# A four-layer graph network on 16 pairs: separate logit products, one bank for a pair's projections, pair-wide transfers and 14 steps given to VectorE

## The chip, the cores and the metric

One Trainium2 chip, one of its NeuronCores. The metric is the time of one execution on the device in microseconds, the median of three runs: 269.04 us (268.43 to 270.58).

## What is computed

The input is x, 32 graphs of 256 nodes with 128 features each, and adj, 32 integer matrices of 256 x 256 with entries 0 and 1. Four layers follow one another, each added to its input and normalized over the features:

```python
def _L0_gnn_ref(x, adj, W, a_src, a_dst):
    h = jnp.einsum('bnf,of->bno', x, W)
    e = (h @ a_src)[:, :, None] + (h @ a_dst)[:, None, :]
    e = jnp.where(adj == 0, NEG_INF, jax.nn.leaky_relu(e, negative_slope=0.2))
    return jnp.einsum('bij,bjo->bio', jax.nn.softmax(e, axis=-1), h)
...
x = _layernorm(x + _L0_gnn_ref(x, adj, L0_gnn_W, L0_gnn_a_src, L0_gnn_a_dst), axis=-1)
x = _layernorm(x + _L1_gnn_ref(x, adj, L1_gnn_W, L1_gnn_a), axis=-1)
x = _layernorm(x + _L2_gnn_ref(x, adj, L2_gnn_a0, L2_gnn_a1, L2_gnn_a2, L2_gnn_a3, L2_gnn_bias), axis=-1)
x = _layernorm(x + _L3_gnn_ref(x, L3_gnn_adj, adj, L3_gnn_weight, L3_gnn_bias), axis=-1)
```

Layer 1 is like layer 0 with other weights. Layer 2 takes sigmoid(leaky(x a x')) as its matrix wherever adj has the value of the relation, layer 3 multiplies the adjacency of each relation with x and that with the relation's weights. Since adj holds only 0 and 1, the kernel computes one relation in layers 2 and 3, keeps note of any other entry (`seen`), and has a general path behind a branch that these inputs don't take.

## The kernel before

The 32 graphs are worked in 16 pairs ("teams", `H = 2`). For each pair a chain of some thirty steps runs over four layers; each step is a small function of one engine, and all steps are written out by hand in `ORDER`, one string per engine: `h0:5` is the step `h` of layer 0 for pair 5. An engine takes its string from left to right and never overtakes. Before each step it waits on semaphores for the steps of other engines whose result it needs, eight semaphores per engine (`K = 8`), so pairs n and n+8 share one. `BANKS` says which of the 8 PSUM banks each product uses, and `bank_free` (L979) makes PE wait for the step that last read the bank (`freed_by`, L972). Rings of buffers (`X_IN`, `XT_IN`, `ADJ`, ...) limit how far a pair may run ahead.

The steps around the change, in the order of one pair:
- SyncE (`load_xT`, `load_x`, `load_adj`, L454 to L471): three loads for each of the two graphs, x laid out by nodes, x turned, the adjacency turned; behind the ninth entry of its string three loads of later weights (L482), all four relations' weights and two biases broadcast to 128 partitions. ScalarE's queue loads W0, the eight attention columns, the turned W0, and W1 (L545 to L548).
- PE `h` (`projections`, L1000): for each graph and each half of 128 nodes one f32 product with the 128x128 block of turned x as stationary and `w_fast` of 130 columns as moving operand, 128 of features and 2 of logits. Each graph has a bank of its own, so a pair holds two. `w_fast` of layer 0 is made from W0 by a product with two columns (L966), that of layer 1 from W1 less its mean (`projection_centre`, L685, and L969, L970).
- VectorE `logits` (L721): takes the two logit columns out of the bank, an instruction for each graph. PE `dT` (L1016) turns them, VectorE `peak` takes the largest, PE `top` (L1020) spreads it, VectorE `dmax`, `shift` subtract it, ScalarE `gains` take two exponentials. `dT` and `top` write into the free columns of the bank of the pair's first projection. ScalarE `vals` (L572) copies the features out of the bank, which is then free.
- PE `rows` (L1029), VectorE `weight` (L760), PE `out` (L1070), VectorE `rsum`, `rinv`, `res` (L799), `stats` (L806), `var`; GpSimd `pow` (L525) for the reciprocal root; ScalarE `norm` (L610; L620 in layer 1, L623 in layers 2 and 3).
- Layer 2: PE `xT`, ScalarE `xTa`, PE `score` (L1037, L1038), ScalarE `sigmoid` (L597, L598), VectorE `alpha` (L767), PE `out`. VectorE adds (L791) what GpSimd `bias` (L521) made of x and the bias. Layer 3: ScalarE `high` (L603) and GpSimd `low` (L530) split x into two f16 parts, PE `agg` (L1047) gathers them, ScalarE copies (L608), PE `out` (L1067).
- VectorE `raw` (L712), `seen` (L719) and ScalarE `mask` (L555) turn the loaded adjacency into what the layers use. SyncE `store` (L473) writes each graph when its `norm3` is done.

The lines that set the cost of a projection are

```python
last = nc.tensor.matmul(place(f"h{l}", u)[:, b * HC:(b + 1) * HC], (xT_in if l == "0" else fxT)(u)[:, b * P:(b + 1) * P], w_fast[:, int(l), :],
                        start=True, stop=True)
```

## Time and profile before

| | us |
|---|---|
| runs, median (lowest, highest) | 269.04 (268.43, 270.58) |
| profiled execution | 270.16 |
| its span, first to last instruction | 268.3 |
| busy in it: VectorE / TensorE / ScalarE / GpSimd | 240.3 / 234.8 / 224.7 / 147.5 |

All times below are microseconds from the start of the profiled span unless marked ns. Engines: PE is TensorE, PEld its weight loads, which overlap it, DVE VectorE, ACT ScalarE, POOL GpSimd, SPq the queue on which SyncE issues DMAs. L1012 is line 1012 of the kernel. `x8` counts instructions of one form that follow each other; the time beside them runs from the first start to the last end. In square brackets stands how long the engine was idle before, and for whom it waited. PEclk is the share of TensorE's clock that was granted.

### The profile page before, as it was taken

The numbers are of one execution on the slowest core, as the hardware profiler recorded it, in microseconds if no ns is written. First come the engines' busy times: TensorE is split into PE (matmuls) and PEld (weight loads), VectorE is DVE, ScalarE is ACT, GpSimd is POOL, SyncE is SP. The second block draws the span as 40 slices with busy tenths as digits, with TensorE's granted clock in tenths as the row PEclk, the third lists the DMA queues.
The fourth block names the chain that finished last, engine by engine and source line by source line (L and its number), as shares of the span: only waits on it lengthen the run. The fifth ranks groups of instructions, "written<-read, shape, count | busy, mean of one in ns | idle before, by whom it ended". The sixth has DMA issues, their size and how long they took to land.

```text
span 268.3 us, 6075 instructions
## 1 busy us (share of the span) xinstructions
PE 234.8 (88%) x1799; PEld 206.9 (77%) x1799; DVE 240.3 (90%) x917; ACT 224.7 (84%) x656; POOL 147.5 (55%) x167
## 2 busy tenths in 40 slices
PE   1796789999999999898899999999999989988960
PEld 1685578798878988788887888988989878877740
DVE  1886999999999899999999999999899998996481
ACT  2431855898989899889997999899899979999984
POOL 1002111605946456866196344798632697899992
PEclk9979999999999999999999999999999999999995
DMA  6979190021280402831106101500020100010114
GB/s 183 366 64 279 42 300 16 19 99 42 78 277 3 120 0 53 247 133 43 42 2 195 39 2 40 156 4 0 23 98 2 40 4 0 0 42 1 39 50 154
DMA packets 20115, 22.12 MB, mean 82 GB/s; under 512 B 2288, under 2 KB 15984, under 8 KB 20080
## 3 DMA queue, kind: packets, MB, share of 16 engines
q1 hardware_dynamic: 19504, 21.50, 27.0%
q8 instruction: 16, 0.26, 0.4%
q10 hardware_dynamic: 576, 0.20, 0.3%
q14 instruction: 19, 0.16, 0.2%
HBM read 17.50 MB, written 4.19 MB: 81 GB/s over the span
## 4 chain that ended last, share of the span: by engine, by line
DVE 54%; POOL 12%; PE 9%; ACT 8%; issue 8%; DMA 6%; SPq 1%; ACTq 1%; DVEq 0%; POOLq 0%
DVE wgt_all L760 12%; DVE fstats L806 9%; DVE fres L799 8%; POOL frstd L525 5%; POOL xb L521 4%; DMA x_in<-x_laid 4%; DVE wgt_all L767 4%; DVE fres L791 4%; DVE raw_all L712 3%; POOL fxTa L530 2%; DVE seen L719 2%; PE banks L1012 2%; ACT xs L623 2%; ACT vals_all L579 2%; DMA w_nat<-in_L_gnn_W 2%
## 5 line engine op out<-in xcount | busy, mean ns | idle before, releaser
L525 POOL TENSOR_TENSOR frstd<-fvar,minus_half 128x4 f32<-128x4 f32 x64 | 75.2, 1179 | 103.1 <-DVE fvar L812 46.6
L1070 PE MATMUL banks<-vals_all,wgt_all 128*128 128x129 f32 x512 | 63.1, 279 | 2.9 <-DVE wgt_all L760 2.9
L1070 PEld LDWEIGHTS banks<-vals_all,wgt_all 128*128 128x128 f32 x512 | 60.2, 194 | 3.8 <-issue 3.0
L760 DVE SCALAR_TENSOR_TENSOR wgt_all<-banks,gain,maskT 128x256 f32<-128x256 f32 x128 | 52.4, 474 | 0.5 <-PE banks L1029 0.3
L806 DVE BATCH_NORM_STATS2 fstats<-fres 128x6 f32<-128x256 f32 x128 | 47.7, 415 | 0.0
L623 ACT ACTIVATE xs<-fres,frstd 128x128 f32<-128x128 f32 x128 | 41.0, 413 | 1.2 <-POOL frstd L525 1.1
L1037 PE MATMUL banks<-fxT,fxTa 128*128 128x256 f32 x128 | 36.1, 384 | 0.1
L1070 PE MATMUL banks<-xs,wgt_all 128*128 128x128 f32 x256 | 32.0, 278 | 0.3
L1070 PEld LDWEIGHTS banks<-xs,wgt_all 128*128 128x128 f32 x256 | 29.9, 192 | 1.5 <-issue 1.2
L562 ACT COPY fxT<-banks 128x256 f32<-128x256 f32 x64 | 20.6, 392 | 10.9 <-PE banks L997 10.9
L791 DVE TENSOR_TENSOR fres<-banks,xb 128x256 f32<-128x256 f32 x64 | 23.7, 412 | 6.6 <-PE banks L1070 3.4
L620 ACT ACTIVATE xs<-fres,fcenter,frstd 128x128 f32<-128x128 f32 x64 | 26.5, 494 | 3.6 <-DVE fcenter L823 3.1
L530 POOL TENSOR_TENSOR fxTa<-xs,fxTa 128x256 f16<-128x256 f32 x32 | 23.0, 739 | 9.5 <-ACT fxTa L603 9.5
L521 POOL TENSOR_TENSOR xb<-xs,bias 128x256 f32<-128x256 f32 x32 | 26.2, 837 | 3.0 <-ACT xs L620 2.9
L521 POOL TENSOR_TENSOR xb<-xs,bias_up 128x256 f32<-128x256 f32 x32 | 24.1, 776 | 0.0
L1037 PEld LDWEIGHTS banks<-fxT,fxTa 128*128 128x128 f32 x128 | 19.3, 191 | 6.0 <-issue 0.3
L767 DVE TENSOR_TENSOR wgt_all<-sg_all,wgt_all 128x512 f32<-128x512 f32 x32 | 22.9, 749 | 1.2 <-ACT wgt_all L598 1.2
L579 ACT ACTIVATE vals_all<-banks,fscale 128x128 f32<-128x128 f32 x64 | 18.4, 383 | 4.8 <-DVE fscale L750 4.6
L1029 PE MATMUL banks<-ident,gain 128*128 128x128 f32 x128 | 19.5, 281 | 2.5 <-ACT vals_all L570 1.6
L1012 PE MATMUL banks<-w_fast,xT_in 128*128 128x130 f32 x128 | 19.1, 295 | 2.1 <-issue 1.6
L555 ACT CAST maskT<-adj_in 128x512 bf16<-128x512 int32 x32 | 18.4, 650 | 2.5 <-DMA adj_in<-adj_turned 2.4
L799 DVE SCALAR_TENSOR_TENSOR fres<-banks,finv,x_in 128x128 f32<-128x128 f32 x64 | 18.0, 341 | 2.4 <-DMA x_in<-x_laid 2.2
(92 smaller groups left out, 448.6 us busy)
## 6 DMA issues: line engine op xcount, KB each, us to landing
adj_in<-adj_turned SPq DMA_DIRECT2D x32, 256.0 KB, 3.8
xT_in<-x_turned SPq DMA_DIRECT2D x32, 128.0 KB, 3.3
x_in<-x_laid SPq DMA_DIRECT2D x32, 128.0 KB, 3.4
out<-xs SPq DMA_DIRECT2D x32, 128.0 KB, 1.7
w<-in_L_gnn_weight SPq DMA_DIRECT2D x1, 256.0 KB, 3.9
bias<-in_L_gnn_bias SPq DMA_DIRECT2D x2, 128.0 KB, 9.4
w_nat<-in_L_gnn_W ACTq DMA_DIRECT2D x2, 64.0 KB, 3.8
w_fast<-W_turned ACTq DMA_DIRECT2D x1, 64.0 KB, 4.4
```

The source lines that it names most:

```text
L521: nc.gpsimd.tensor_tensor(xb(u)[:, :, :], xs(u)[:, :, :], bias_up[:, :, :] if l == "3" else bias[:, 0, :, :], ALU.add).then_inc(fast_pool[ ...
L525: nc.gpsimd.tensor_tensor(frstd[:, int(l), slot(n), :], fvar[:, int(l), slot(n), :], minus_half[:, :, :], ALU.pow).then_inc(fast_pool[k], 1)
L530: nc.gpsimd.tensor_tensor(lo(u)[:, :, :], xs(u)[:, :, :], hi(u)[:, :, :], ALU.subtract).then_inc(fast_pool[k], 1)
L620: last = nc.scalar.activation(xs(u)[:, b, :], fres(u)[:, b, :], ACT.Identity, bias=fcenter[:, u, b:b + 1], scale=frstd[:, 1, u, b:b + 1])
L623: last = nc.scalar.activation(xs(u)[:, b, :], fres(u)[:, b, :], ACT.Copy, scale=frstd[:, int(l), u, b:b + 1])
L760: last = nc.vector.scalar_tensor_tensor(out=wgt(u)[:, c, :], in0=place(f"rows{l}", u), scalar=gain[:, u, c, 1:2], in1=maskT(u)[:, c, :], o ...
L767: nc.vector.tensor_tensor(wgt(u), sg(u), wgt(u), ALU.max).then_inc(fast_dve[k], 1)
L791: nc.vector.tensor_tensor(fres(u)[:, :, :], place(f"out{l}", u).rearrange("p (b c) -> p b c", b=NB), xb(u)[:, :, :], ALU.add).then_inc(fas ...
L799: last = nc.vector.scalar_tensor_tensor(out=fres(u)[:, b, :], in0=sums[:, b, 0:D], scalar=finv[:, u, b:b + 1], in1=(x_in if l == "0" else ...
L806: nc.vector.bn_stats(fstats[:, u, :, :].rearrange("p b k -> p (b k)"), fres(u)[:, :, :].rearrange("p b d -> p d b")).then_inc(fast_dve[k], 1)
L1037: nc.tensor.matmul(place("score", u)[:, c * N:(c + 1) * N], fxTa(u)[:, c * P:(c + 1) * P], fxT(u)[:, :], start=True, stop=False)
L1070: last = nc.tensor.matmul(place(f"out{l}", u)[:, b * width:(b + 1) * width], wgt(u)[:, c, b * P:(b + 1) * P], (vals if l in "01" else xs)( ...
```

## The change

The logits get products of their own: a step `lg` multiplies the same stationary blocks of turned x with the last two columns of `w_fast`, all four products of a pair into one bank, in which `dT` and `top` also work. The projection `h` moves 128 columns only, both graphs of a pair into one bank; it no longer stands between x and the logits, and its result is needed by `vals` alone. `logits` takes the four columns pairs with one instruction.

Loads and stores move a pair at a time, from inputs laid out for it. W0 and the eight columns come as one load. The biases are laid out for 128 partitions beforehand and come as one load, and of layer 3's weights only the used relation; both stand behind the twelfth entry of SyncE's string. The mean of W1 is taken after the first `shift` and the weights of layer 1 are made before the first `weight` (PE: before the first `rows`).

VectorE gets versions of `mask`, `bias`, `low` and `norm`, and 14 steps of other engines now stand in its string: `mask:10`, `norm2` of 5, 8, 11, 12, 14, `norm3` of 10, 14 (from ScalarE), `low` of 9, 13, 14, 15, `bias2:15`, `bias3:12` (from GpSimd). Waits for such a step ask `doer` which engine has it. All five strings and `BANKS` are written anew. In ScalarE's string the runs of `gains` and of `sigmoid` alternate 18 times, before 16 times.

```diff
 ORDER = {
     "sp": (
-        "xT:0 adj:0 adj:1 xT:1 adj:2 xT:2 adj:3 x:0 xT:3 x:1 adj:4 x:2 xT:5 adj:5 x:4 adj:6 adj:7 x:3 xT:4 x:6 x:5 "
-        "adj:8 xT:6 xT:9 x:9 adj:11 xT:7 adj:9 xT:8 adj:10 adj:12 x:7 xT:12 xT:11 x:10 xT:10 x:8 adj:14 adj:13 x:11 "
...
+        "xT:0 xT:2 xT:1 adj:0 adj:1 xT:3 x:0 adj:2 xT:4 xT:5 adj:4 x:2 adj:5 adj:3 x:1 xT:6 x:4 adj:6 xT:7 adj:7 "
+        "adj:8 x:5 x:6 x:3 adj:9 xT:10 adj:12 x:9 adj:11 xT:9 xT:8 x:7 adj:10 adj:13 x:8 xT:11 store:1 store:0 "
...
     "pe": (
-        "h0:0 dT0:0 h0:1 top0:0 dT0:1 top0:1 rows0:0 rows0:1 out0:0 out0:1 xT1:0 h0:2 h1:0 dT0:2 xT1:1 h0:3 dT1:0 "
...
+        "lg0:0 h0:0 dT0:0 lg0:2 lg0:1 top0:0 dT0:1 top0:1 dT0:2 rows0:0 h0:1 h0:2 rows0:1 out0:0 lg0:3 lg0:4 h0:4 "
+        "dT0:3 dT0:4 top0:2 xT1:0 h0:3 top0:3 top0:4 lg1:0 h1:0 dT1:0 out0:1 top1:0 lg0:5 rows0:2 rows1:0 out0:2 "
...
     "dve": (
-        "raw:0 logits0:0 peak0:0 raw:1 seen:0 seen:1 logits0:1 dmax0:0 shift0:0 peak0:1 dmax0:1 raw:2 shift0:1 "
...
+        "logits0:0 peak0:0 logits0:1 dmax0:0 shift0:0 logits0:2 peak0:1 raw:0 dmax0:1 seen:0 shift0:1 raw:1 weight0:0 "
+        "weight0:1 rsum0:0 raw:2 logits0:3 logits0:4 rinv0:0 peak0:2 res0:0 peak0:3 stats0:0 peak0:4 var0:0 dmax0:2 "
...
+        "res2:15 stats2:15 low:13 var2:15 res3:11 alpha:14 stats3:11 var3:11 res2:14 stats2:14 var2:14 low:15 res3:12 "
+        "norm2:14 stats3:12 low:14 res3:13 var3:12 stats3:13 res3:15 var3:13 stats3:15 var3:15 res3:14 stats3:14 "
+        "var3:14 norm3:14"
...
-    "h0": "01 23 23 40 16 23 71 75 40 32 67 67 32 73 46 67",
...
+    "h0": "1 5 6 3 7 3 4 6 6 2 4 0 1 2 1 0",
+    "lg0": "0 3 2 4 5 5 7 6 4 2 5 0 3 7 0 6",
...
-PHASES = {"h0": H, "rows0": 1, "out0": H, "xT1": 1, "h1": H, "rows1": 1, "out1": H,
+PHASES = {"lg0": 1, "h0": 1, "rows0": 1, "out0": H, "xT1": 1, "lg1": 1, "h1": 1, "rows1": 1, "out1": H,
...
-        loads = [
-            (w3[:, :, :], W3.rearrange("r d o -> d r o")),
-        ]
-        for k, bb in ((0, bias2), (1, bias3)):
-            loads.append((bias[:, k, :, :], bb.rearrange("(a c d) -> a c d", a=1, c=1).to_broadcast([P, NB, D])))
+        loads = [(bias[:, :, 0, :], biases_laid), (w3[:, 0, :], W3[0])]
         WEIGHTS = 16 * len(loads)
+        LOADS_AFTER = FIRST_LOADS
...
             def load_xT(l, n, k):
-                for u in graphs(n):
-                    if n >= XT_IN:
-                        sp.wait_ge(fast_pe[(n - XT_IN) % K], at("pe", "h0", u - XT_IN * H))
-                    sp.dma_start(xT_in(u)[:, :], x_turned[u]).then_inc(fast_xT_in[u % (XT_IN * H)], 16)
+                if n >= XT_IN:
+                    sp.wait_ge(fast_pe[(n - XT_IN) % K], max(at("pe", "h0", final(n - XT_IN)), at("pe", "lg0", final(n - XT_IN))))
+                sp.dma_start(xT_all[:, pair(n, XT_IN), :], x_turned[n]).then_inc(fast_xT_in[n % XT_IN], 16)
...
             def store(l, n, k):
-                for u in graphs(n):
-                    sp.wait_ge(fast_act[k], at("act", "norm3", u))
-                    sp.dma_start(out[u], xs(u)[:, :, :]).then_inc(fast_stored[n % XS], 16)
+                normer = doer("norm3", n)
+                sp.wait_ge(signals[normer][k], at(normer, "norm3", final(n)))
+                sp.dma_start(out[n * H:(n + 1) * H].rearrange("h p b d -> p h b d"), xs_all[:, pair(n, XS), :, :]).then_inc(fast_stored[n % XS], 16)
...
-            act.dma_start(w_nat[:, 0, :], W0).then_inc(w0_in, 16)
-            act.dma_start(columns[:, :], vector_columns).then_inc(columns_in, 16)
+            act.dma_start(w0_pack[:, :], W0_and_columns).then_inc(w0_in, 16)
             act.dma_start(w_fast[:, 0, 0:D], W0_turned).then_inc(w0_turned_in, 16)
-            act.dma_start(w_nat[:, 1, :], W1).then_inc(w1_in, 16)
+            act.dma_start(w1_nat[:, :], W1).then_inc(w1_in, 16)
...
+            def normalize(l, n, k):
+                dve.wait_ge(fast_pool[k], at("pool", f"pow{l}", n * H))
+                for u in graphs(n):
+                    for b in range(NB):
+                        last = nc.vector.tensor_scalar(xs(u)[:, b, :], fres(u)[:, b, :], frstd[:, int(l), u, b:b + 1], None, ALU.mult)
+                    last.then_inc(fast_dve[k], 1)
...
+                if f"lg{l}" in PHASES:
+                    parts = chain_place(l, n)[:, 0:H * NB * 2]
+                    if l == "0":
+                        nc.vector.tensor_copy(logit[:, 0, slot(n), :, :].rearrange("p u b k -> p (u b k)"), parts).then_inc(fast_dve[k], 1)
+                    else:
+                        nc.vector.tensor_tensor(logit[:, 1, slot(n), :, :].rearrange("p u b k -> p (u b) k"), parts.rearrange("p (c k) -> p c k", k=2),
+                                                frstd[:, 0, slot(n), :].rearrange("p u (b a) -> p (u b) a", a=1).to_broadcast([P, H * NB, 2]), ALU.mult).then_inc(fast_dve[k], 1)
+                    return
...
                 if q == 0:
                     projection_weights(0)
-                    projection_centre()
+                if q == first_weight:
+                    projection_weights(1)
                 if q == finished:
                     output_weights()
                 steps[step](l, n, n % K)
-                if q == first_logits:
-                    projection_weights(1)
+                if q == first_shift:
+                    projection_centre()
...
+                    width = HC if PHASES[f"h{l}"] == H else D
                     for b in range(NB):
-                        last = nc.tensor.matmul(place(f"h{l}", u)[:, b * HC:(b + 1) * HC], (xT_in if l == "0" else fxT)(u)[:, b * P:(b + 1) * P], w_fast[:, int(l), :],
+                        last = nc.tensor.matmul(place(f"h{l}", u)[:, b * width:(b + 1) * width], (xT_in if l == "0" else fxT)(u)[:, b * P:(b + 1) * P], w_fast[:, int(l), 0:width],
...
+            def logit_products(l, n, k):
+                if n == first("pe", f"lg{l}"):
+                    pe.wait_ge(w_fast_set, int(l) + 1)
+                bank_free(f"lg{l}", n * H)
+                if l == "0":
+                    pe.wait_ge(fast_xT_in[n % XT_IN], loaded(n * H, XT_IN))
+                else:
+                    pe.wait_ge(fast_act[k], at("act", "xT1", final(n)))
+                for u in graphs(n):
+                    for b in range(NB):
+                        column = u % H * NB * 2 + b * 2
+                        last = nc.tensor.matmul(chain_place(l, n)[:, column:column + 2], (xT_in if l == "0" else fxT)(u)[:, b * P:(b + 1) * P], w_fast[:, int(l), D:HC],
+                                                start=True, stop=True)
+                last.then_inc(fast_pe[k], 1)
+
...
+            first_rows = next(q for q, step in enumerate(sequence) if step[0] == "rows")
             projection_weights(0)
             for q, (step, l, n) in enumerate(sequence):
+                if q == first_rows:
+                    projection_weights(1)
                 steps[step](l, n, n % K)
-                if q == projected:
-                    projection_weights(1)
```

## Rows read from the trace of the kernel before

**Rows 1.** The page, part 1: busy time, share of the span, instructions, by engine.
```profile
PE 234.8 (88%) x1799; PEld 206.9 (77%) x1799; DVE 240.3 (90%) x917; ACT 224.7 (84%) x656; POOL 147.5 (55%) x167
```

**Rows 2.** The span in stages: length, then busy time (and instructions) by engine, PEclk, DMA share, GB/s.
```profile
0.00:30.00 30.00, 19.49 (x122) 16.74 (x123) 19.86 (x85) 11.37 (x35) 3.41 (x9) 0.94 0.78 209
30.00:225.00 195.00, 183.25 (x1435) 163.11 (x1436) 190.59 (x743) 175.75 (x516) 107.87 (x115) 1.00 0.23 72
225.00:262.00 37.00, 31.86 (x243) 26.96 (x241) 28.98 (x88) 34.76 (x99) 35.04 (x43) 1.00 0.08 26
```

**Rows 3.** The chain that ended last, 225 to 268 us: start, length, what.
```profile
225.37 1.30 POOL fxTa L530 x2
...
230.19 2.78 POOL xb L521 x4
232.98 1.39 POOL frstd L525
```

**Rows 4.** Two short stretches at the start, as in rows 2.
```profile
13.40:20.00 6.60, 5.97 (x38) 5.60 (x38) 5.47 (x20) 2.36 (x10) 0.00 (x0) 0.74 0.80 64
20.00:25.00 5.00, 2.71 (x22) 2.25 (x21) 2.82 (x14) 0.65 (x2) 1.03 (x1) 1.00 0.89 257
```

**Rows 5.** The chain that ended last, 9 to 26 us.
```profile
12.56 11.31 DMA x_in<-x_laid
```

**Rows 6.** The page, part 6: DMA issues, KB each, median us to landing.
```profile
x_in<-x_laid SPq DMA_DIRECT2D x32, 128.0 KB, 3.4
...
bias<-in_L_gnn_bias SPq DMA_DIRECT2D x2, 128.0 KB, 9.4
```

**Rows 7.** Groups by line and form: busy us, mean ns of one, idle before.
```profile
L1012 PE MATMUL banks<-w_fast,fxT 128*128 128x130 f32 x128 | 18.0, 282 | 1.2 <-ACT wgt_all L598 0.7 <-ACT fxT L562 0.6
...
L1012 PEld LDWEIGHTS banks<-w_fast,fxT 128*128 128x128 f32 x128 | 15.7, 190 | 2.1 <-ACT wgt_all L598 0.9 <-ACT fxT L562 0.5 <-DVE fstats L806 0.5
...
L1047 PEld LDWEIGHTS banks<-maskT,fxTa 128*128 128x128 f16 x128 | 11.7, 97 | 4.8 <-issue 1.9 <-POOL fxTa L530 1.1 <-ACT vals_all L579 0.2
...
L730 DVE TENSOR_TENSOR logit<-banks,frstd 128x4 f32<-128x4 f32 x32 | 3.5, 150 | 0.3 <-PE banks L1012 0.2
...
L683 DVE TENSOR_SCALAR w_cen<-w_nat,mean_mv 128x128 f32<-128x128 f32 x1 | 0.3, 286 | 0.0
...
L791 DVE TENSOR_TENSOR fres<-banks,xb 128x256 f32<-128x256 f32 x64 | 23.7, 412 | 6.6 <-PE banks L1070 3.4 <-PE banks L1067 3.2
...
L712 DVE TENSOR_SCALAR raw_all<-adj_in 128x512 bf16<-128x512 int32 x32 | 13.0, 447 | 0.0
...
L623 ACT ACTIVATE xs<-fres,frstd 128x128 f32<-128x128 f32 x128 | 41.0, 413 | 1.2 <-POOL frstd L525 1.1
...
L597 ACT ACT_TABLE_LOAD x8 | 10.3, 1283 | 0.1
```

**Rows 8.** Timeline, TensorE and its loads: start, length, instructions.
```profile
99.72 0.60 PE L1037 MATMUL banks<-fxT,fxTa 128*128 128x256 f32 x2
...
101.45 0.21 PE L1022 MATMUL banks<-ident,top 4*128 4x4 f32 x1
...
101.59 2.05 PE L1070 MATMUL banks<-vals_all,wgt_all 128*128 128x129 f32 x16
...
104.90 0.97 PEld L1067 LDWEIGHTS banks<-w_cen,fxT 128*128 128x128 f32 x8
105.01 1.05 PE L1067 MATMUL banks<-w_cen,fxT 128*128 128x128 f32 x8
```

**Rows 9.** The middle stage, two lines of TensorE alone.
```profile
30.00:225.00 195.00, 28.99 (x208) 25.45 (x208) 1.00 0.23 72
...
30.00:225.00 195.00, 29.32 (x104) 15.68 (x104) 1.00 0.23 72
```

**Rows 10.** Timeline, the first TensorE work.
```profile
4.05 0.56 PE L966 MATMUL banks<-columns,w_nat 128*128 128x2 f32 x2 [4.05 <-DMA columns<-vector_columns]
...
6.17 2.07 PE L1012 MATMUL banks<-w_fast,xT_in 128*128 128x130 f32 x8 [1.57 <-issue]
```

204 lines of the change are left out of this document (127 added, 77 removed), and 187 rows, old and new, of tables (BANKS, ORDER).

## The prediction

> **What bounds the kernel now.** I read the sums of busy time first, then the span in stages, then the chain of work that ended last in the two stages whose time the sums don't explain, and last the forms and single starts of TensorE's passes.
>
> The sums put two engines near the span of 268.3 us: VectorE (DVE) 240.3 us and TensorE (PE) 234.8; ScalarE (ACT) has 224.7, GpSimd (POOL) 147.5 [rows 1]. The stages show where each counts. From 30 to 225 us, 195 us long, VectorE is busy 190.6 us, 97.7%: it is the bound there, with PE at 183.3 and ACT at 175.8 [rows 2]. From 225 to 262 VectorE has only 29.0 of 37, but POOL 35.0 and ACT 34.8 [rows 2], and the chain of that stage goes from POOL step to POOL step (`bias`, `pow`, `low`) [rows 3]. In the first 30 us nothing is full: VectorE 19.9, ACT 11.4 [rows 2]. The hole is from 20 to 25 us, VectorE 2.82 and ACT 0.65 of 5.00 [rows 4]; the chain across it is one load of x, issued at 12.56 and landed 11.31 us later [rows 5]. The usual load of x takes 3.4 us; just ahead of this one on SyncE's queue stand the two bias broadcasts, 9.4 us each to landing [rows 6], and from 13.4 to 20 us the DMA engines are 80% busy for 64 GB/s [rows 4].
>
> PE's busy time flatters it, since rows overlap, so I turn it into occupation. An f32 matmul is two passes: the 64 projections of one layer are 128 rows of L1012 [rows 7]. A row lasts 0.28 us, but most of that is pipeline: 8 passes of 128 columns take 1.05 us, so they start (1.05-0.28)/7 = 0.111 us apart [rows 8]; for 256 columns I take twice that, 0.22. From 30 to 225 there are 1435 passes, 104 of them of 256 columns [rows 2, 9]: 1331 x 0.111 + 104 x 0.22 = 170.6 us, 87.5% of the stage. PE has 24 us of room there.
>
> **The logit products.** Each `lg` step adds 4 matmuls that move 2 columns past a full 128x128 stationary block: 8 passes, as a two-column product is two passes too (L966: one matmul, 2 rows) [rows 10]. 32 steps make 256 passes; the 256 passes of `h` stay and lose 2 of 130 columns, about 0.002 us each, 0.4 us in all. What does a two-column pass cost? The warm part of the trace has no row of one. At the slow pace of the start eight wide passes take 2.07 us, 0.26 each, and the two narrow ones of L966 0.56, 0.28 each [rows 10]: a narrow pass is no cheaper than a wide one there. And weight loads alone follow each other at the same 0.111 us (8 in 0.97, of 0.19 each) [rows 7, 8]. I take 0.111 us: 256 x 0.111 = 28.4 us more on PE. Upper end 0.14, the distance from a lone four-column product to the next step (101.45 to 101.59) [rows 8]: 36 us. Lower end half of 0.111, since the loads of half the bytes take half the time (0.097 against 0.190) [rows 7]: 14 us. A cost of nothing is excluded for seven of eight passes: only the first load of a step can hide behind the wide pass before it.
>
> The Trainium skill speaks to this twice. "TensorE: Matmul & The Clock Gate", section "LDWEIGHTS (loading the stationary operand)", has a load take its columns over 1.2, here 107 ns whatever is moved; the load spacing of [rows 8] agrees, and the sum would be 27.4 us. The same page, "Back-to-back issue gap", gives 1 to 64 columns about 60 cycles, and its Part 2 lets loads run ahead of matmuls in flight: by that the 256 passes would cost 6.4 us. No row here shows narrow passes that close; it is the third rival's rule.
>
> Of the 256 projection passes 208 lie in the middle stage [rows 9]; with as many of `lg` it gets 23.1 us more: 193.7 us of PE in 195. The slack that would have hidden them is used up. VectorE's own bill hardly moves. It loses 32 of 64 `logits` instructions at 0.109 us (3.5 us over 32) [rows 7], 2.8 us of it in this stage. It gains `mask:10` (2 x 0.41, as L712), `norm2:5` and `norm2:8` (4 pieces each) and `low:9` (2 x 0.37, as L791). A `norm` piece, 128 columns from SBUF to SBUF, has one near form on VectorE, L683 at 0.286 alone; bounds 0.15 and 0.286, and back to back I take 0.22 [rows 7]. Gains 3.4 us, so 191.2 us. Two engines now want 194 and 191 us of one stage, in orders written down beforehand, each waiting for the other. VectorE as the one bound reached 97.7%; I take 96.5% for PE: 193.7/0.965 = 200.7 us, so the middle grows by **5.7 us**. Bounds: 100% gives -1.3, 93% gives +13.3.
>
> One bank for a pair's projections and one for its chain, in place of two held from `h` to `vals`: `h` may come later and banks turn over sooner. I price it at 0 (-2 to +1), inside the 96.5%.
>
> **The start.** Of the weights for layer 3 only the used quarter is loaded; the two broadcasts of 128 KB [rows 6] become one laid-out 128 KB; all move from place 9 to 12 of SyncE's order, ahead of x:1 as before. Without the jam x:1 should land in some 4 us instead of 11.3. VectorE idles 6.60+5.00-5.47-2.82 = 3.3 us from 13.4 to 25 us [rows 4]; most goes, and VectorE's early stop for W1's load may go too, as the centring moves behind the first shift. Against that, `h0:0` and two further `lg` steps now stand between the first x and the first `top`, each 2 us at the early pace [rows 10]. Pair-wide transfers halve SyncE's issues, but a pair's first graph waits for its second: 131 KB at 257 GB/s [rows 4] is 0.5 us; even. Start: **-3.5 us**, bounds -6 and 0.
>
> **The end.** `bias2:15`, `bias3:12` and `low:13` to `low:15` leave POOL: 4 x 0.70 and 6 x 0.65, 6.7 us [rows 3] of the 35.0. Five norm steps leave ACT: 20 x 0.32 = 6.4 us [rows 7] of the 34.8. All land on VectorE: 10 x 0.37 and 20 x 0.22 are 8.1 us on top of 29.0, 37.1 in a stage of 37 [rows 2, 7]. The old bound is gone, the next is level with it: **-1.5 us**, bounds -6 and +2. A pair's store waits for its second graph, 0.6 us, and saves an issue; 0. ACT's `gains` and `sigmoid` change places 18 times instead of 16, each a table load of 1.28 us [rows 7]; the 2.6 us hide in ACT's 19 us of idle time in the middle, and would cost in full without it.
>
> **Sum.** The profiled execution took 270.16 us (span 268.3 and 1.9 around it), 1.1 above the median of 269.04. The terms are differences, so I set them on the median: 269.04 - 3.5 + 5.7 - 1.5 = **269.7 us**. A measurement of this kernel can tell about 1% from no change.
>
> **Rivals.**
> 1. *TensorE becomes the bound and stalls as well.* Place: the middle. Its passes fill 93% instead of 96.5%: 208.3 us, +13.3; total 269.04 - 3.5 + 13.3 - 1.5 = 277.3. It decides from 95% down (203.9 us, total 273). For it: each `dT` and `top` is a round trip through VectorE, now between two nearly full engines. Against: the orders keep some eight teams in flight.
> 2. *The transfers don't help.* On SyncE's queue x:1 stands behind adj:5 and adj:3, which wait for `raw` and `mask` of pairs 2 and 0, so it may be late without any jam: the start's 3.5 us stay, 273.2. Against: 64 GB/s at 80% busy is a jam of its own.
> 3. *Narrow products are cheap and the relief counts in full.* At half price the middle wants 182.2 us of PE, VectorE is the bound again at 191.2/0.977 = 195.7, +0.7; start -4.5, end -3.5: 261.7. By the skill's gap rule it would be this case too. Against: [rows 8, 10].
>
> **How the numbers follow.** Forecast 0.42, its own range 266 to 273; rival 1 0.27; rival 3 0.26; rival 2 0.05. The forecast gives 0.04 to faster by over 1% (under 266.3), 0.28 to within, 0.10 to slower (over 271.7); rival 3 is all faster, rival 1 all slower, rival 2 0.01 within and 0.04 slower: faster 0.30, same 0.29, slower 0.41. For eight in ten the far parts of rivals 1 and 3 are cut off: 261 to 279.
>
> **What would show it.** PE has 256 rows more, some 2055, and 20 to 28 us more busy time; the passes of the new line start 0.11 us apart. In the middle PE is 97% busy or more and VectorE below 96%. No x load takes over 6 us before 30 us, and VectorE has over 4 of the 5 us from 20 to 25. POOL's chain at the end is replaced by VectorE's steps. I am wrong if the new passes are 0.06 us apart or closer, if VectorE stays at 98% in the middle, or if the end shrinks by more than 4 us.

## The result, and the profile after

| | before | after |
|---|---|---|
| median of 4 runs on one chip (lowest to highest) | 269.12 us (268.43 to 270.58) | 286.93 us (285.96 to 290.82) |
| profiled execution, its span | 270.16, 268.3 us | 285.96, 284.1 us |

The ratio is 1.063 [1.059, 1.067]: 6% slower, 17.8 us by the medians and 15.8 by the two profiled executions, where the forecast had 269.7 us and a range that ended at 279. Of the four executions after, three took 285.96 to 287.06 us; the fourth, 290.82, was in a slower state at a lower clock.

The page of the kernel after, its busy times and two groups of the new line (busy us, mean ns of one, idle before):

```profile
PE 259.5 (91%) x2055; PEld 238.2 (84%) x2055; DVE 249.8 (88%) x928; ACT 218.7 (77%) x628; POOL 136.1 (48%) x155
```
```profile
L1102 PE MATMUL banks<-w_fast,xT_all 128*128 128x2 f32 x128 | 17.8, 263 | 1.6 <-DMA xT_all<-x_turned 1.3 <-DVE w_fast L720 0.3
L1102 PE MATMUL banks<-w_fast,fxT 128*128 128x2 f32 x128 | 15.6, 244 | 0.4 <-ACT fxT L586 0.4
```

TensorE (PE) has its 256 rows more and 24.7 us more busy time [against rows 1]; eight narrow passes at full pace last 1.02 us, 0.11 apart. The chain that ended last is now 61% PE and 23% VectorE (DVE). The span in the stages of [rows 2], the last one longer:

```profile
0.00:30.00 30.00, 24.90 (x163) 23.54 (x163) 16.66 (x68) 11.36 (x31) 2.80 (x8) 1.00 0.62 215
30.00:225.00 195.00, 188.72 (x1539) 174.86 (x1540) 180.57 (x684) 163.03 (x473) 95.75 (x107) 0.99 0.20 67
225.00:278.00 53.00, 45.64 (x355) 39.71 (x354) 51.08 (x174) 42.56 (x120) 36.32 (x39) 1.00 0.05 17
```

The middle looks as forecast: PE 96.8% busy, VectorE 92.6%, down from 97.7%. But fixed windows of two kernels no longer hold the same work. So I set TensorE's passes side by side: both kernels have the same 1799 passes apart from the narrow ones, though not in the same order. The table has the start of the k-th such pass, and how much later it starts in the changed kernel and in some of the runs below (in brackets the narrow passes done by then).

| k-th pass | before, us | after | 256 added | 80 early | 176 late | transfers alone |
|---|---|---|---|---|---|---|
| 50 | 17.7 | +1.6 (24) | +3.3 (16) | +3.0 (16) | +0.8 (0) | +1.1 |
| 125 | 30.4 | +2.9 (56) | +3.7 (48) | +3.4 (48) | -0.7 (0) | -1.3 |
| 225 | 45.9 | +7.5 (80) | +6.8 (72) | +5.7 (64) | +1.2 (8) | +0.1 |
| 825 | 126.9 | +10.9 (176) | +10.6 (160) | +6.2 (80) | +3.7 (80) | +0.4 |
| 1525 | 218.8 | +15.4 (256) | +16.1 (256) | +6.2 (80) | +9.2 (176) | +0.4 |
| last | 262.1 | +15.9 (256) | +15.4 (256) | +6.1 (80) | +8.1 (176) | -0.3 |

Each column is one execution. The kernel of `176 late` is the kernel before up to its first narrow pass, and yet stands 0.8 us behind it at pass 50, 0.7 ahead at 125 and 0.7 behind at 200, so an entry is good to about 1 us.

Half of the loss stands at 46 us, with less than a third of the narrow passes done. The chain of waits of the first 26 us shows why:

```profile
4.47 1.87 PE banks L1102 x8
6.34 1.92 PE banks L1087 x8
...
8.47 3.21 PE banks L1102 x16
11.68 0.21 PE banks L1112
```

The first pair's peak (L1112, `top`) stands behind 24 narrow and 8 wide passes, and each narrow one takes 0.20 to 0.23 us there, twice its later pace. That pace isn't theirs alone. Two rows of wide passes, sixteen and then eight:

```profile
15.09 3.01 PE L1087 MATMUL banks<-w_fast,xT_all 128*128 128x128 f32 x16
...
23.85 1.06 PE L1087 MATMUL banks<-w_fast,xT_all 128*128 128x128 f32 x8
```

Until 17.3 us passes of the changed kernel that follow each other start 0.213 us apart, the pace of its later rows at half clock, and 0.111 behind. The trace has no record of the clock before 17.3 us; the 1.00 that windows print for that time is no measurement. In the kernel before, passes come down to 0.111 at 10.0 us, where its record begins, and are back at 0.214 only from 13.9 to 16.8. So the changed kernel did its first passes, 24 narrow ones among them, at the slow pace for longer.

The bias jam is gone, and TensorE has taken its place, full where [rows 4] had 2.71 of 5.00:

```profile
13.40:20.00 6.60, 6.60 (x44) 6.58 (x45) 5.35 (x18) 4.71 (x15) 0.00 (x0) 1.00 0.19 53
20.00:25.00 5.00, 5.00 (x44) 4.54 (x43) 4.16 (x20) 0.95 (x3) 0.20 (x1) 1.00 1.03 374
```

The x load of pair 1, which the forecast wanted early, was in fact issued only at 22.1 us (before at 12.6) and took 6.4 us to land, later than before the change. It was late without a jam, as the second rival had it, though not for its reason: SyncE stood 7.4 us at xT:4, whose buffer comes free with TensorE's `h0:1`, and 0.5 at the adjacency. No engine waited for the load.

Then comes a hole. First TensorE's timeline, then VectorE's:

```profile
33.77 0.61 PE L1161 MATMUL banks<-vals_all,wgt_all 128*128 128x129 f32 x4
37.61 3.61 PE L1161 MATMUL banks<-vals_all,wgt_all 128*128 128x129 f32 x16 [3.23 <-DVE wgt_all L829]
```
```profile
33.78 0.27 DVE L705 BATCH_NORM_STATS2 mean_stats<-w 128x6 f32<-128x128 f32 x1
...
36.38 0.29 DVE L734 COPY bias_cen<-bias_cen 128x256 f32<-128x256 f32 x1
36.59 1.65 DVE L829 SCALAR_TENSOR_TENSOR wgt_all<-banks,gain,maskT 128x256 f32<-128x256 f32 x4
```

From 33.78 to 36.6 us VectorE centres W3 and the biases (`output_weights`, L705 to L734) ahead of the edge weights that TensorE waits for. When TensorE resumes, 16 passes take 3.61 us, at full clock 2.05 (as at 32.33 us): the granted clock is at 1.2 instead of 2.4 GHz.

```profile
34.00:38.00 4.00, 0.77 (x7) 0.61 (x6) 3.70 (x18) 1.86 (x9) 0.00 (x0) 0.97 0.84 283
38.00:41.00 3.00, 3.00 (x15) 2.92 (x15) 1.72 (x7) 0.00 (x0) 0.00 (x0) 0.50 0.83 307
```

### The profile page after: what moved, and what is told of

Its sections match the earlier page's. It is cut to its first block, busy times and chain, and to the rows that moved or that the text cites. A ratio compares the mean times of both kernels' runs of the same rounds, so it can differ in the third digit from the quotient of the medians.

```text
span 284.1 us, 6530 instructions
## 1 busy us (share of the span) xinstructions
PE 259.5 (91%) x2055; PEld 238.2 (84%) x2055; DVE 249.8 (88%) x928; ACT 218.7 (77%) x628; POOL 136.1 (48%) x155
## 3 DMA queue, kind: packets, MB, share of 16 engines
q1 hardware_dynamic: 11680, 21.17, 22.1%
## 4 chain that ended last, share of the span: by engine, by line
PE 61%; DVE 23%; ACT 5%; issue 4%; DMA 3%; POOL 2%; SPq 0%; DVEq 0%; ACTq 0%; POOLq 0%
PE banks L1161 19%; PE banks L1087 9%; PE banks L1102 8%; PE banks L1127 6%; PE banks L1070 4%; DVE fstats L877 4%; PE banks L1158 4%; PE banks L1119 4%; DVE wgt_all L829 3%; PE banks L1138 3%; DVE fres L870 3%; DVE fres L862 3%; DMA xT_all<-x_turned 2%; DVE wgt_all L836 2%; ACT xs_all L647 2%
## 5 line engine op out<-in xcount | busy, mean ns | idle before, releaser
L546 POOL TENSOR_TENSOR xb<-xs_all,bias_cen 128x256 f32<-128x256 f32 x60 | 46.3, 793 | 2.1 <-ACT xs_all L647 1.7
L586 ACT COPY fxT<-banks 128x256 f32<-128x256 f32 x64 | 21.0, 393 | 22.1 <-PE banks L1070 22.1
L1161 PE MATMUL banks<-xs_all,wgt_all 128*128 128x128 f32 x256 | 32.4, 279 | 2.0 <-DVE wgt_all L836 1.9
L650 ACT ACTIVATE xs_all<-fres,frstd 128x128 f32<-128x128 f32 x100 | 31.9, 407 | 2.6 <-POOL frstd L550 2.5
L1161 PEld LDWEIGHTS banks<-xs_all,wgt_all 128*128 128x128 f32 x256 | 30.0, 192 | 3.7 <-issue 3.1
L647 ACT ACTIVATE xs_all<-fres,fcenter,frstd 128x128 f32<-128x128 f32 x64 | 26.4, 493 | 6.8 <-DVE fcenter L894 6.7
L623 ACT ACTIVATE sg_all<-banks 128x512 f32<-128x512 f32 x32 | 19.3, 602 | 3.8 <-PE banks L1128 3.6
L555 POOL TENSOR_TENSOR fxTa<-xs_all,fxTa 128x256 f16<-128x256 f32 x24 | 17.6, 753 | 7.0 <-ACT fxTa L630 7.0
L1102 PEld LDWEIGHTS banks<-w_fast,xT_all 128*128 128x128 f32 x128 | 17.9, 218 | 2.1 <-DVE fsum L845 1.4
L1087 PE MATMUL banks<-w_fast,xT_all 128*128 128x128 f32 x128 | 19.4, 301 | 0.0
L624 ACT ACTIVATE wgt_all<-banks 128x512 f32<-128x512 f32 x32 | 19.3, 604 | 0.0
```

What stands on the lines that cost most here:

```text
L546: nc.gpsimd.tensor_tensor(xb(u)[:, :, :], xs(u)[:, :, :], bias_cen[:, int(l) - 2, :, :], ALU.add).then_inc(fast_pool[k], 1)
L647: last = nc.scalar.activation(xs(u)[:, b, :], fres(u)[:, b, :], ACT.Identity, bias=fcenter[:, u, b:b + 1], scale=frstd[:, 1, u, b:b + 1])
L650: last = nc.scalar.activation(xs(u)[:, b, :], fres(u)[:, b, :], ACT.Copy, scale=frstd[:, int(l), u, b:b + 1])
L1087: last = nc.tensor.matmul(place(f"h{l}", u)[:, b * width:(b + 1) * width], (xT_in if l == "0" else fxT)(u)[:, b * P:(b + 1) * P], w_fast[: ...
L1102: last = nc.tensor.matmul(chain_place(l, n)[:, column:column + 2], (xT_in if l == "0" else fxT)(u)[:, b * P:(b + 1) * P], w_fast[:, int(l) ...
L1161: last = nc.tensor.matmul(place(f"out{l}", u)[:, b * width:(b + 1) * width], wgt(u)[:, c, b * P:(b + 1) * P], (vals if l in "01" else xs)( ...
```

## The experiments

Three theories: the *passes* (256 f32 passes at full price, whatever else changed), the *plan* (transfers, orders, banks, steps moved), and *lumps* (stretches of VectorE's own work that leave TensorE dry and its clock at half). The theories A, B and C named below are those of each run's own expectation. The before of each run is that of its own chip, 269.6 to 270.4 us.

**e_transfers**: the changed kernel with `ORDER`, `BANKS` and `PHASES` of before; what is left of the change is the transfers, the biases laid out beforehand, and the later place of the work on W1.

```diff
-PHASES = {"lg0": 1, "h0": 1, "rows0": 1, "out0": H, "xT1": 1, "lg1": 1, "h1": 1,
+PHASES = {"h0": H, "rows0": 1, "out0": H, "xT1": 1, "h1": H,
-FIRST_LOADS = 12
+FIRST_LOADS = 9
```

> The transfers and the laid-out biases alone: the changed code with the strings and banks of before, logits taken from the projections, nothing moved to VectorE, later weights behind the ninth entry of SyncE's string. Theory A (TensorE's 256 added passes are the loss; the start's jam was real and worth 3.5 us): 264 to 267 us. Theory B (pair-wide loads and a pair's late first graph cost as much as the jam did): 268.5 to 270. If it is over 275 the loss lies in the transfers and not in the plan.

Measured: 269.40 us, ratio 0.9965 [0.9936, 0.9994]; theory B's number. Its windows:

```profile
13.40:20.00 6.60, 6.41 (x33) 5.88 (x32) 4.54 (x17) 2.26 (x10) 0.00 (x0) 1.00 0.28 107
20.00:25.00 5.00, 4.98 (x42) 4.25 (x41) 5.00 (x24) 1.29 (x4) 1.32 (x2) 1.00 0.33 106
30.00:34.00 4.00, 1.64 (x11) 1.47 (x10) 3.77 (x22) 1.98 (x4) 0.00 (x0) 0.88 0.20 66
34.00:37.00 3.00, 3.00 (x19) 3.00 (x18) 2.89 (x14) 0.50 (x4) 0.32 (x1) 0.60 0.95 369
```

The hole of [rows 4] is filled, VectorE 5.00 of 5.00, and yet TensorE is only 1.3 us ahead at 30 us (2.1 at pass 100 in g_weights below, which is the same kernel up to there; its passes come to the full pace at 16.8 us, those of e_transfers at 19.4). By 36 us that is gone: TensorE waits for over half of 30 to 34 us, while VectorE is nearly full, and then works at a lower clock.

**e_added**: the kernel before with 256 narrow passes, read by nobody.

```diff
+                    for b in range(NB):
+                        last = nc.tensor.matmul(place(f"h{l}", u)[:, 500 + 2 * b:502 + 2 * b], (xT_in if l == "0" else fxT)(u)[:, b * P:(b + 1) * P], w_fast[:, int(l), D:HC],
+                                                start=True, stop=True)
```

> The kernel before with nothing changed but 2 two-column products more for each graph behind each projection, 256 passes in all, into free columns of the projection's own bank; nobody reads them. Theory A: each pass takes 0.111 us of TensorE, whose room in the middle (24 us) they fill, and they stand in the chain ahead of the logits: 278 to 288 us, with TensorE over 97% busy from 50 to 150 us. Theory C (passes are cheap, the new order and banks are the loss): under 273 us.

Measured: 285.17 us, 1.054 [1.047, 1.062], theory A. Its new line:

```profile
L1015 PE MATMUL banks<-w_fast,xT_in 128*128 128x2 f32 x128 | 17.5, 241 | 0.0
L1015 PE MATMUL banks<-w_fast,fxT 128*128 128x2 f32 x128 | 16.1, 231 | 0.0
```

Nothing of the change is in this kernel but the passes, and it is 15.1 us slower; its column of the table follows that of the change. The passes account for some 15 of the 17.8 us.

**g_late** and **h_early**: the same in two parts, `range(NB if n >= 5 else 0)` and `range(NB if n < 5 else 0)`.

> The kernel before with the two-column float32 products added beside the projections of pairs 5 to 15 alone, 176 passes of the 256; nobody reads their results. With all 256 the time was 285.2 us, 15.1 over before, of which 6.8 us stood on TensorE's progress by 46 us with 72 passes done, and 8.6 us behind it with 184. Theory A (the price of a pass hangs on its place: nearly the whole 0.1 us in the first 46 us, where chains of few pairs run through TensorE and no other pair's work covers it, 0.047 us behind, where VectorE's waits hid about half of it): 270.1 + 176 x 0.047 = 278.4 us, 277.5 to 279.3. Theory B (every pass costs alike, 0.059 us): 280.5 us, 279.8 to 281.2. Theory C (late passes cost next to nothing until the early ones have used up TensorE's slack): under 276 us.

> The kernel before with the two-column float32 products added beside the projections of pairs 0 to 4 alone, 80 passes of the 256, the other part of the run with the 176; nobody reads their results. That run took 278.2 us, 7.8 us over before for 176 passes, or 0.044 us a pass. Theory A (a pass of the first 46 us costs nearly its whole time on TensorE, 0.085 to 0.11 us, and what it costs there is not won back behind): 80 x 0.085 to 0.11 = 6.8 to 8.8 us, 277 to 279.2 us. Theory B (early delays are absorbed behind, where TensorE has slack, as the win of the transfers was given back): under 274 us. If A holds, the two parts, run apart, add up to the 15.1 us of the run with all 256.

Measured: 278.18 us for the 176 late passes, 1.031 [1.027, 1.036], and 278.40 for the 80 early ones, 1.028 [1.021, 1.035]; 7.8 and 8.2 us, together 16.0 against 15.1 with all. Theory A holds for both. A late pass costs 0.044 us. For an early one the median says 0.10, the table 6.1/80 = 0.076; the other 2.2 us are the last store, which took 4.0 us to land in the profiled execution against 1.7 before (one of the four executions, 276.23 us, was that much shorter; why the store took longer is open). The price of an early pass isn't the pass alone: in e_added and h_early the slow pace of the start lasts until 21.3 us, and from 38.2 to 41.7 us the clock is at half, where the kernel before kept 1.00. No run parts the two. An early delay is not caught up behind: the column stays at 6.2 from pass 825 to the end.

**e_quarter**: the changed kernel with 64 narrow passes; it leaves out the logits of three of four blocks of nodes.

```diff
-                for u in graphs(n):
-                    for b in range(NB):
...
+                u = n * H
+                last = nc.tensor.matmul(chain_place(l, n)[:, 0:8].rearrange("p (c k) -> p c k", k=2), (xT_in if l == "0" else fxT)(u)[:, 0:P],
+                                        w_fast[:, int(l), D:HC].rearrange("p (a k) -> p a k", a=1).to_broadcast([P, 4, 2]), start=True, stop=True)
```

> The changed kernel with one product per lg step instead of four, 8 columns of the first block only, so 64 passes instead of 256; three of four logit blocks are left out (they repeat the first). Orders and banks are the changed kernel's. Theory A: 192 passes fewer at 0.111 us, 21 us of a bound engine, of which 80 to 100% come back: 266 to 271 us, and VectorE is the bound again. Theory C: the order itself loses, 277 us or more.

Measured: 272.19 us, 1.012 [1.003, 1.021], between the theories and nearer to A, which ended at 271.

**e_half**: the changed kernel with the narrow products in bf16, one pass each; their operands are rounded.

```diff
-...[:, b * P:(b + 1) * P], w_fast[:, int(l), D:HC],
+...[:, b * P:(b + 1) * P].bitcast(BF16)[:, 1::2], w_fast[:, int(l), D:HC].bitcast(BF16)[:, 1::2],
```

> The changed kernel with the lg products on the upper halves of the f32 words read as bf16, one pass each, 128 instead of 256; the lower halves are left out of the logits. Theory A: 14 us of TensorE fewer if a bf16 pass costs 0.11, more if it is shorter: 272 to 277 us. Theory C: 282 us or more.

Measured: 273.19 us, 1.013 [1.006, 1.020], theory A. The new line in one group, its loads, and four of its passes in the timeline:

```profile
L1102 PE MATMUL banks<-w_fast,fxT 128*128 128x2 bf16 x64 | 3.9, 164 | 0.0
```
```profile
L1102 PEld LDWEIGHTS banks<-w_fast,fxT 128*128 128x128 bf16 x64 | 3.6, 98 | 0.9 <-issue 0.5
```
```profile
61.63 0.24 PE L1102 MATMUL banks<-w_fast,fxT 128*128 128x2 bf16 x4
```

A load is half as long as a float32 one [rows 7], but the passes are closer than half: (0.24 - 0.164)/3 = 0.025 us apart, not the 0.06 that I had divided from the busy time in the expectations. These two runs win 14 us over the changed kernel; the passes carry its loss from this side too. Yet both stay slower than before. TensorE's progress in e_half shows where: 0.8 us ahead of before at pass 1525, 3.0 behind at 1625; e_quarter is 1.7 ahead and 1.1 behind there. In the timeline of e_half and its windows:

```profile
221.16 1.37 PE L1070 MATMUL banks<-ident,xs_all 128*128 128x128 f32 x4 [2.27 <-DVE fsum L845]
```
```profile
218.00:222.00 4.00, 1.71 (x12) 0.92 (x10) 3.86 (x21) 1.86 (x6) 1.17 (x2) 0.86 0.01 2
222.00:226.00 4.00, 4.00 (x16) 3.29 (x17) 3.79 (x20) 3.17 (x13) 1.10 (x2) 0.50 0.01 4
```

Again a lump of VectorE: from 217.1 to 220.0 us it judges the ranges (`judge`), TensorE waits 2.27 us, and at 222 to 226 its clock is at half.

**f_added_half**: e_added with bf16 operands as in e_half, 128 passes.

> The kernel before with 128 two-column products more, beside each projection, as in the run that added 256 passes in float32, but with both operands read as bf16 (the upper halves), so that each is one pass; their results are read by nobody. Theory A (the price is that of passes on TensorE, and a bf16 pass takes 0.06 us where a float32 one takes 0.111): 128 x 0.06 = 7.7 us of TensorE instead of 28.4, which the kernel before, with 96% in its middle for VectorE and TensorE at about 84%, hides but for a little: 270 to 272.5 us. Theory B (the price is in the products' being there, a semaphore or the switch between float32 and bf16, not in their pace): over 277 us.

Measured: 271.30 us, 1.005 [1.002, 1.008]. Theory A, with passes even cheaper than it has them: 128 x 0.025 is 3.2 us of TensorE. The same products cost 15.1 us of time in float32 and 1.2 in bf16.

**f_start**: the order of the first 22 us alone.

```diff
-        "lg0:0 h0:0 dT0:0 lg0:2 lg0:1 top0:0 dT0:1 top0:1 dT0:2 rows0:0 h0:1 h0:2 rows0:1 out0:0
+        "lg0:0 h0:0 dT0:0 lg0:1 top0:0 dT0:1 rows0:0 top0:1 h0:1 rows0:1 lg0:2 h0:2 dT0:2 out0:0
-        "logits0:0 peak0:0 logits0:1 dmax0:0 shift0:0 logits0:2 peak0:1 raw:0 dmax0:1 seen:0 shift0:1 raw:1 weight0:0 weight0:1 rsum0:0
+        "logits0:0 peak0:0 logits0:1 dmax0:0 shift0:0 peak0:1 raw:0 dmax0:1 seen:0 shift0:1 raw:1 weight0:0 weight0:1 logits0:2 rsum0:0
```

> The changed kernel with the order of the first 22 us alone altered: TensorE's gather and spread of the first pair's peak follow its products at once, and the logits of the pairs 1 and 2 (16 two-column products each pair of graphs' worth, 3.2 us between 8.3 and 11.6 us) come behind them, those of pair 2 behind the first pair's row spreads. The same passes are all issued. Theory A (the start's loss of 2.9 us against the kernel before, at TensorE's 125th pass of the other kind, is the placing of these narrow products ahead of the first pair's chain): the first spread comes at 8.7 instead of 11.6 us, the first edge weights 1.5 to 3 us earlier, and 284 to 285.5 us in all. Theory B (the number of TensorE's passes sets the start too; what is moved is only done later): the first edge weights come earlier, but at 30 us TensorE is where it was, and 286.3 to 287.3 us in all.

Measured: 286.96 us, 1.065 [1.059, 1.071], no change; theory B. Of the two `lg` steps ahead of the first `top` the edit moves one, that of pair 2; so `top` comes at 9.93 us and not at the 8.7 of the expectation, 1.7 us earlier than in the changed kernel. The eight narrow passes that made room are back at 15.58:

```profile
9.93 0.26 PE L1113 MATMUL banks<-ident,top 4*128 4x4 f32 x1
...
15.58 0.95 PE L1103 MATMUL banks<-w_fast,xT_all 128*128 128x2 f32 x8
```

At pass 125 it is 3.2 us behind before, the changed kernel 2.9. Moving eight of the narrow passes behind the first pair's chain won nothing that lasted; what the other eight cost where they stand is not tested.

**f_weights** and **g_weights**: `output_weights` behind the edge weights instead of ahead of them, in the changed kernel and in e_transfers.

```diff
-            finished = next(q for q, step in enumerate(sequence) if step[:2] == ("weight", "1"))
+            finished = next(q for q, step in enumerate(sequence) if step[:2] == ("rsum", "1"))
```

> The changed kernel with one move on VectorE: the centring of W3 and the two biases (2.9 us of VectorE, at 33.8 to 36.6 in the changed kernel) stands no more ahead of the first pair's edge weights of layer 2, for which TensorE stood 3.23 us at 37.6, but behind them and the steps that follow, ahead of the first row sums of layer 2, where VectorE itself was idle for 1.53 us. All is still computed. Theory A (TensorE bounds this kernel from 30 us to 262 us, so that every hole of TensorE that is closed ahead of it comes off the end): TensorE goes on 1.5 to 3 us earlier at 37 us, and the time falls by as much, to 284 to 285.5 us. Theory B (the steps after it are late for other reasons, and the gain is taken back by 50 us as that of the transfers was): 286.3 to 287.3 us. A rise would say that the biases or W3 are then late for the pair's later layers.

> The kernel with the transfers of the change and the steps' order of before (269.4 us), and in it the centring of W3 and the biases moved on VectorE from 29.2 to 32.0 us, ahead of the first edge weights of layer 2, to behind them, ahead of the first row sums of layer 2. In that kernel TensorE stood over half of 30 to 34 us, and its granted clock was 0.5 from 32.5 to 36.4 us; the 1.3 us that the transfers had won by 30 us were gone by 42 us. Theory A (the hole and the half clock behind it take the gain): without them the win stays, 267.5 to 268.5 us. Theory B (another wait follows at once, VectorE has as much to do in these 20 us whatever the order): TensorE's hole and the fall of the clock come a few us later instead, as they did with this move in the changed kernel, and 269 to 271 us.

Measured: f_weights 289.17 us, 1.076 [1.068, 1.083], slower than the change and outside both theories; g_weights 270.19 us, 1.0003 [0.998, 1.003], theory B: TensorE's hole comes at 34 to 38 us instead (1.63 of 4 us busy), the half clock from 37.3. At pass 150 f_weights was 4.9 us ahead of the change, at pass 225 3.1 behind. Its windows, and its narrow passes at that clock:

```profile
34.00:41.00 7.00, 4.90 (x37) 4.40 (x38) 6.70 (x34) 2.07 (x9) 1.01 (x1) 0.96 0.87 294
41.00:54.00 13.00, 13.00 (x61) 12.12 (x60) 6.62 (x29) 5.40 (x16) 2.02 (x2) 0.50 0.15 45
```
```profile
46.22 1.87 PE L1102 MATMUL banks<-w_fast,fxT 128*128 128x2 f32 x8
```

TensorE's idle time was only moved, to 37 to 41 us, and the half clock behind it lasted 13 us instead of 3.4. Each pass takes twice as long there, 1.87 us for eight instead of 1.02, and VectorE is half idle. Late biases, which the expectation named for such a rise, are not the cause there: TensorE is busy 13.00 of 13.00 us.

**f_best**: e_half with the start of f_start and the move of f_weights.

> The changed kernel with three edits together: the logits' products in bf16 (one pass each, 128 instead of 256), the centring of W3 and the biases moved as in the second run of this call's kind, and the first 22 us in the altered order. All outputs are still computed, the logits with operands rounded to bf16. The run with the bf16 products alone took 273.2 us. Theory A (with TensorE relieved, each hole of the first 50 us comes off the time): 269 to 271.5 us, level with the kernel before. Theory B (VectorE, busy 91% of that run, is the bound, so that holes of TensorE cost nothing any more): 272.5 to 273.7 us.

Measured: 272.61 us, 1.009 [1.006, 1.013]: theory B's number. It too has its clock at half, from 39.2 to 46.0 us.

**g_tail**: the changed kernel with eight steps of the last 30 us given back: `bias2:15`, `bias3:12`, `low:13` to `low:15` to GpSimd (POOL), `norm2:12`, `norm2:14`, `norm3:14` to ScalarE.

```diff
     "dve": (
-        ... "bias2:15" ... "norm2:12 bias3:12" ... "low:13" ... "low:15" ... "norm2:14" ... "low:14" ... "norm3:14"
     "pool": (
-        "... bias2:14 pow2:12 pow2:13 bias3:11 bias3:13 pow2:15 low:12 pow3:11 pow2:14 bias3:15 bias3:14 pow3:12 ..."
+        "... bias2:14 bias2:15 pow2:12 pow2:13 bias3:11 bias3:12 bias3:13 pow2:15 low:12 low:13 pow3:11 pow2:14 bias3:15 low:15 bias3:14 low:14 pow3:12 ..."
```

> The changed kernel with eight of VectorE's steps in the last 30 us given back to the engines that did them before: the biases of pairs 15 (layer 3) and 12 (layer 4) and the low parts of 13, 14, 15 to POOL, the scalings by the deviation of pairs 12 and 14 (layer 3) and 14 (layer 4) to ScalarE. Nothing is left out. Theory A (the forecast's own step: moved to VectorE these were to win 1.5 us at the end, as VectorE does each in half of POOL's time): given back they cost that, 288 to 289 us. Theory B (in the changed kernel VectorE ends the chain, 87% busy from 255 us on, and the steps given to it lie on it): 1 to 3 us less, 284 to 286 us. Theory C (the end goes by the chain of a pair, and either engine does it in the same time): 286.5 to 287.5 us.

Measured: 296.85 us, 1.097 [1.092, 1.101], 9.9 us over the change; no theory had so much. Its profiled execution took 300.9 us, more than the three at 296.1 to 296.9, so that its trace holds some 4 us that they don't. Until the 1700th pass (245.5 us before) it is 4.2 us behind that of the change, most of it lost around a stretch at half clock from 46 to 56 us; this may belong to that execution alone. The last hundred passes add 9.8, as much as the medians differ. There POOL is the chain:

```profile
252.00:274.00 22.00, 15.10 (x106) 12.20 (x105) 16.36 (x38) 18.17 (x49) 20.68 (x26) 0.93 0.04 13
```
```profile
267.70 2.09 POOL xb L547 x3
269.79 1.42 POOL frstd L551
271.21 2.52 POOL fxTa L556 x4
```

So theory A's sign holds: in this plan the moved steps do relieve the end. The table has it that the end as a whole gained nothing over before (+15.4 at pass 1625, 15.8 on the span).

**i_after**, **i_half**, **i_before**, **i_transfers**: the two lumps cut up in four kernels.

```diff
-                if q == finished:
-                    output_weights()
...
-                if q == judged:
-                    judge()
+                if q - finished in (0, 4, 8, 11, 14):
+                    output_weights((0, 4, 8, 11, 14).index(q - finished))
+                if q - judged in (12, 16, 20, 24, 28, 32):
+                    judge((12, 16, 20, 24, 28, 32).index(q - judged))
```

> The changed kernel with VectorE's two lumps cut up: the centring of W3 and the biases in five pieces, behind the first edge weights of layer 2 and then one behind every third or fourth step, and the judging of ranges in six pieces, from twelve steps behind its old place on, one every four steps. All is computed. Theory A (the lumps leave TensorE dry, 3.23 us at 37.6, and its clock at half for 3.4 us behind): 2 to 4 us less, 283 to 285 us. Theory B (TensorE has as many passes to do, and dry spells only move): 286.3 to 288 us.

> The same cuts in the kernel with the logits' products in bf16 (273.2 us), where the judging at 217 us left TensorE 2.27 us idle at 221 us and 6.6 us at half clock behind it, and TensorE's progress fell from 0.8 us ahead of the kernel before to 3.0 behind between 219 and 234 us. Theory A: both losses go, 268.5 to 270.5 us. Theory B (VectorE bounds this kernel, and its steps only change places): 272.5 to 273.7 us.

> The kernel before with the same cuts: the centring in four pieces, the judging in six, from fourteen steps behind its old place on, into the stretch in which VectorE is idle for 4.7 of 12 us (240 to 252). Theory A (the judging leaves the full middle for the empty end, and TensorE's idle 2.24 us at 34 us goes): 1 to 3 us less than before, 267 to 269 us. Theory B (the end's chain of the last pairs takes it up): 269.5 to 270.8 us.

> The same cuts in the kernel with the change's transfers and the steps' order of before (269.4 us). Theory A (the 1.3 to 2.1 us that TensorE is ahead at 30 us are kept, as neither the dry spell at 30 to 34 us nor the half clock behind it comes, and the judging moves into the empty end): 266 to 268 us. Theory B: 269 to 270 us.

Measured: i_after 288.18 us, 1.069 [1.064, 1.073]; i_half 268.73 us, 0.996 [0.994, 0.999]; i_before 268.32 us, 0.993 [0.991, 0.996]; i_transfers 268.84 us, 0.995 [0.993, 0.997]. Theory A holds for i_half (4.5 us less than e_half; its clock is at half from 28.1 to 31.5 us only, that of e_half from 33.2 to 40.0 and from 220.9 to 227.7) and, at the edge of its range, for i_before; i_transfers ends between its theories: it is 0.8 us below its own before, where e_transfers was 0.65 below its own, so the cut added next to nothing there. i_before's window over the stretch in which [rows 2] had TensorE at 183.3 and VectorE at 190.6:

```profile
30.00:225.00 195.00, 185.04 (x1453) 164.85 (x1453) 188.98 (x740) 178.11 (x522) 109.04 (x119) 1.00 0.23 71
```

It has 18 passes more in it. In the changed kernel itself the effect is not settled: the four executions of i_after took 284.5, 287.0, 289.4 and 289.4 us, on both sides of the change's 286.9. The profiled one is the shortest, and it too kept little of its lead: at pass 150 it is 4.1 us ahead of the change, at pass 225 only 0.6. The dry spell at 34 us is gone, but the clock falls all the same, a little later, and from 38 to 42 us TensorE had been busy 3.56 of 4 us with no wait above 0.4:

```profile
42.00:46.00 4.00, 4.00 (x18) 3.20 (x18) 3.00 (x13) 2.21 (x5) 1.18 (x1) 0.50 0.19 67
```

Three kernels of this study are thus 0.4 to 0.7% faster than before (e_transfers 0.35%), i_half with rounded logits. None of them has the float32 narrow products.

## Why the prediction was wrong

In short: the price of a pass was right, and two steps failed. The start was forecast at -3.5 us, with nothing set down for the `lg` steps that stand in its chain, and came to +2.9; and the middle's added passes were offset against slack that its first 16 us didn't have, so that it grew by 12.5 us and not by 5.7.

**The price of a narrow pass** was right: 0.111 us each, some 28 us of TensorE. Rival 3, which had them cheap, is out for float32; f_added_half shows that it would have been right for bf16. The two rules of the Trainium skill that the forecast weighed ("TensorE: Matmul & The Clock Gate", "LDWEIGHTS (loading the stationary operand)" and "Back-to-back issue gap") each hold for one type here: float32 goes at the pace of the load, 0.111 us against the rule's 107 ns, and the issue floor of about 25 ns for 1 to 64 columns is just what the bf16 passes show, 0.025. The same page's "Weight-path perf modes" says between them: the fast weight load is on for a full block of 128 weights that isn't float32. The rows agree, 98 ns a load against 190; I hadn't brought that section to bear. That the load is what holds a float32 pass back is argued from the equal distances; no run changes the load alone. The forecast's 0.26 and 0.28 us a pass at the start [rows 10] are lengths divided by counts; from start to start both kinds are 0.21 apart.

**The rule of 96.5%** was right as well, where the stage is what it takes it for. From pass 225 to pass 1525 the changed kernel has these rows, first all of TensorE, then the 256-column form and the new one:

```profile
53.40:234.20 180.80, 179.06 (x1478) 166.38 (x1478) 169.52 (x627) 155.97 (x446) 100.34 (x112) 1.00 0.18 58
```
```profile
53.40:234.20 180.80, 26.99 (x96) 14.50 (x96) 1.00 0.18 58
```
```profile
53.40:234.20 180.80, 20.95 (x176) 21.32 (x176) 1.00 0.18 58
```

1382 x 0.111 + 96 x 0.22 is 174.5 us of passes in 180.8, 96.5%. That it fits to the tenth is luck, as the forecast's bounds were 93 and 100%. So rival 1's mechanism, both engines full and TensorE losing time on round trips, took no more than the forecast gave it. That stretch grew by 7.9 us.

**The failed step of the middle** is its pooling: "193.7 us of PE in 195", with the slack of 195 us taken as one. From 30 to 46 us there is none to be had: chains of few pairs, TensorE waiting for single steps. There 24 narrow passes (2.7 us), 1.0 us more of waiting than before had at this place (3.23 against 2.24) and 3.4 us at half clock (1.7) make an estimate of 5.4; measured 4.6. Passes 125 to 1525, about the stage, grew by 4.6 + 7.9 = 12.5 us against the 5.7 of the forecast.

**The failed step of the start** was "-3.5 us, bounds -6 and 0"; measured +2.9 at pass 125. Two things were wrong. The jam was priced by VectorE's idle time, 3.3 us, as if all of it were the load's; e_transfers removes the jam, fills VectorE to 5.00 of 5.00 and wins 1.3 (g_weights 2.1). And the two `lg` steps ahead of the first `top` were named, "each 2 us at the early pace", and then given no term; they took 1.7 us each (sixteen passes at 0.213). The 48 narrow passes that h_early has done by pass 125 cost it 3.4 us; with the 1.3 won that gives +2.1, and 8 more narrow passes stood there. The slow pace until 17.3 us, where the kernel before had left it at 10.0 for the first time, is part of both figures, and no run tells how much. The bound of 0 had nothing to stand on.

**The end**, "-1.5 us": measured +0.4 from pass 1625 to the end of the span. g_tail shows that the moved steps do relieve POOL and ScalarE, and its 9.9 us are more than I would have given; that the new plan needs this relief to end level with the old one I had not seen.

The misses are 6.4 us at the start, 6.8 in the middle, 1.9 at the end, 15.1 in all. The median missed by 17.2; most of the rest is that the profiled execution before lies 1.0 us over its median and the one after 1.0 under. Each miss has the same sign: three terms were taken from sums of busy time, where a chain set the pace. What the range lacked was a case with a start above zero. Bank sharing was priced at 0 and no run tells it apart from the rest of the plan; nor the two more table loads of ScalarE. Rival 2's late load came about and cost nothing, as no engine waited for it.

"What would show it" came out as written for the rows of TensorE, for the middle's shares but for a little (TensorE at 96.8%, not 97 or more), and for VectorE at 4.16 of 5 us from 20 to 25; the sign of the x loads failed, with one of 6.4 us against the 6 named; POOL's chain at the end did give way to VectorE's steps, busy 51.08 of 53 us. All that was true of a kernel 17 us slower than forecast: signs that only tell shares don't tell the time.
